# ScalarE normalises in the prologue, the second layernorm runs in halves, and attention values and sums share a bank

## The chip, the cores and the metric

The kernel runs on one core of one Trainium2 chip. The metric is the device time of one execution in microseconds (us), lower is better; the median of some runs is given. A core has five engines with queues of their own: TensorE (PE; its weight loads are PEld), VectorE (DVE), ScalarE (ACT), GpSimd (POOL) and SyncE (SP), which here only starts transfers. They wait for each other on semaphores alone. SBUF has 128 partitions; PSUM, which TensorE writes, has eight banks of 512 fp32 columns.

## The reference

Four sublayers on x of 4x256x256 (1,024 tokens, 256 wide), each on a layernorm and added back:

```
x = x + L0_xattn(layernorm(x), ctx)      # fp8-rounded activations times fp8-rounded ctx, per batch
x = x + L0_ffn(layernorm(x), ...)        # 32 experts, 4 a token, softmax of the 4 * 1.8, and one shared expert
x = x + L1_xattn(layernorm(x), ctx, ctx, gamma)   # 8 heads of 32, softmax(q k) v, times gamma
x = x + L1_ffn(layernorm(x), ...)        # 8 experts, 2 a token, and a shared expert of twice the width

def layernorm(x):  return (x - mean(x)) / sqrt(var(x) + 1e-5)
```

The first sublayer scales each block of 128 values by 448 over its largest magnitude, rounds to fp8, multiplies by the likewise rounded ctx and scales back. All the rest is fp32.

## The kernel before

x lies as eight tiles (NT) of 128 tokens in `x_sb`, the normalised x in `xn`. All engines' programs are written out by hand, and each engine works through its own in order.

**Prologue (0 to 57 us).** VectorE takes the statistics of x (`statistics`: L604, then L607), the largest magnitudes of ctx, and the inverse deviations of all tiles (`inverse_deviation`, L276 to L283: a Newton iteration of 11 small instructions on VectorE, 14 on POOL, each waiting for the one before). Then it scales ctx (L644) and finds the power of two for the rounding (L626, L627), and signals `c_mag`. POOL, which waits for it, adds and subtracts over 2048 columns (L389, L390): this rounds ctx to `wq`. VectorE meanwhile normalises the eight tiles (L612: one instruction a tile, minus the mean, times the inverse deviation), takes the block maxima of xn (L649, a reduction), then three small instructions (L650 to L652), a scale (L654) and `dq` (L657, eight small products), and rounds xn in two halves (L663, L626, L627, L665, L666). TensorE transposes the rounded halves (L930), ScalarE copies them out (printed at L463), TensorE multiplies (L938), and VectorE adds the scaled products into `x_sb` (L671, four instructions a tile). TensorE's product for tile t waits for tile t-2 there.

**Second layernorm and routing of layer 0 (57 to 110 us).** `layernorm(range(NT), xn_ready)` on VectorE: eight L604, eight L607, the inverse deviations, eight L612. TensorE transposes pairs of tiles (`turn_rows`, L988), ScalarE copies them (`router_copies`, L470) and TensorE makes the logits (L1004, four matmuls a tile); pairs 0 and 1 are turned first, then each next pair between the logits. Then VectorE picks the top four and builds the tables of slots; beside it TensorE, ScalarE and POOL run the first part of the shared expert (L964 up, L953 transposes, L975 down; POOL multiplies at L401 and adds at L406).

**Experts of layer 0 (110 to 252 us).** 48 tiles of 128 rows gathered by POOL's indirect transfers, TensorE busy throughout. Then POOL fetches the rows back (L431).

**Attention (the rows come back from 254 on; heads from 268 to 360 us).** VectorE combines the rows of tile t (L824), takes statistics and normalises; the inverse deviations of groups of two tiles are POOL's, by `by_pool`, whose keys are the heads g after which VectorE takes the statistics (the normalisation follows three heads later). 32 heads, four a tile: `scores` (L1123), the maximum (L848, VectorE), exponential (L560, ScalarE), transposes (`turn_p`, L1135), copy (L567, ScalarE). `values(t)` is four heads' values into bank 6 (L1148) and their sums into bank 7 (L1153). `tile_out(t)` on VectorE takes the reciprocal of the sums (L853), the product with gamma and the values (L855, signals `att_ready`) and adds to x (L858). `values(t)` waits for `att_ready` of t-1. In VectorE's order `tile_out(t)` stands after the maximum of head 4t+10 and before that of head 4t+11. The last two tiles' layernorm is VectorE's alone, and the routing of layer 1 begins.

**Experts of layer 1 (390 to 447 us)**, then rows back and the last combine.

## Time and profile before

| | us |
|---|---|
| median of 3 runs | 480.09 (478.62 to 483.44) |
| profiled execution | 486.58, span 484.8 |
| prologue, until x1 is complete | 57 |
| second layernorm and logits | 57 to 74 |
| routing and shared expert | 74 to 110 |
| experts of layer 0, rows back | 110 to 317 (the attention begins at about 268 within it) |
| rest of the attention | 317 to 360 |
| layer 1's experts | 360 to 485 |

A row of the timeline gives start and length in us, the engine, the line, the operation, what it writes and reads, how often, and in brackets how long the engine had stood idle and for whom. A piece of the chain gives start, length, engine, what is written and the line: it is what the end of the kernel hung on. Where several instructions stand in one row, its length runs from the first start to the last end.

### The profile page before, as it was taken

Reading aid. Unit: us, or ns where it says so; the run is one execution under the profiler, and the core shown is the slowest. Engines: PE = TensorE matmul, PEld = TensorE weight load, DVE = VectorE, ACT = ScalarE, POOL = GpSimd, SP = SyncE. Lnnn points to the kernel's source line nnn. Section 1 sums busy time; section 2 is a strip of 40 time slices with the busy share of each in tenths; the row PEclk is TensorE's granted clock in tenths of the full one; section 3 lists DMA queues with packets and bytes.
Section 4 is the critical chain, followed back from the end, with each engine's and each line's share of the span. In section 5 each row is a group of like instructions: output and inputs, shape, how many; then the busy total and the mean of one; then the engine's idle time right before and its main releaser. Section 6 shows DMA issues by size and latency. Waiting matters only on the chain.

```text
span 484.8 us, 8137 instructions
## 1 busy us (share of the span) xinstructions
PE 364.0 (75%) x2329; PEld 206.9 (43%) x2329; DVE 292.9 (60%) x807; ACT 179.3 (37%) x378; POOL 150.7 (31%) x219
## 2 busy tenths in 40 slices
PE   0002376789999999999960766888767989998993
PEld 0001174454545455455520434555454545544562
DVE  3999837933555555555544786678658235555273
ACT  1000030325555555555530434455612155553230
POOL 2250001443333333333106654542200433320362
PEclk9999999999999999999995557959865599999997
DMA  8998980054222222235522321296020113331242
GB/s 251 343 329 184 355 214 2 0 150 155 89 92 95 96 91 88 91 92 136 164 87 76 87 78 32 77 280 170 1 88 0 43 47 100 96 88 55 65 121 88
DMA packets 33371, 56.92 MB, mean 117 GB/s; under 512 B 4193, under 2 KB 20065, under 8 KB 33329
## 3 DMA queue, kind: packets, MB, share of 16 engines
q1 hardware_dynamic: 26145, 40.08, 26.8%
q0 software_dynamic: 5568, 15.21, 11.5%
q10 hardware_dynamic: 1616, 1.11, 0.8%
q8 instruction: 21, 0.34, 0.3%
q14 instruction: 21, 0.17, 0.1%
HBM read 44.33 MB, written 12.06 MB: 116 GB/s over the span
## 4 chain that ended last, share of the span: by engine, by line
PE 55%; DVE 20%; DMA 15%; issue 5%; POOL 3%; ACT 1%; DVEq 0%; SPq 0%; POOLq 0%; ACTq 0%
PE bank L1056 19%; DMA arena<-m_ys,back 13%; PE bank L1077 12%; PE bank L1067 5%; PE bank L964 4%; PE bank L1051 3%; DVE xn L612 3%; PE bank L975 2%; DVE arena L853 2%; PE bank L1004 2%; DVE st L604 2%; DVE x_sb L671 1%; DMA x_sb<-x 1%; POOL arena L431 1%; PE bank L953 1%
## 5 line engine op out<-in xcount | busy, mean ns | idle before, releaser
L1056 PE MATMUL bank<-arena,xT 128*64 x272 | 111.2, 491 | 1.1 <-ACT xT L528 1.1
L1059 PE MATMUL bank<-xn,xT 128*64 128x384 f32 (+1 forms) x272 | 111.2, 491 | 0.0
L418 POOL DMA_INDIRECT xg<-m_xn,tab x68 | 64.5, 949 | 121.6 <-PE bank L1051 118.9
L1077 PE MATMUL bank<-arena,hT 96*64 (+1 forms) x272 | 70.3, 380 | 2.8 <-DVE hT L792 2.7
L1080 PE MATMUL bank<-xn,hT 96*64 96x256 f32 (+1 forms) x272 | 70.4, 381 | 0.0
L431 POOL DMA_INDIRECT arena<-m_ys,back x48 | 47.5, 990 | 69.9 <-DMA m_ys<-ysb 40.5
L521 ACT ACTIVATE xn<-arena 128x768 f32 (+1 forms) x68 | 56.2, 827 | 22.0 <-issue 22.0
L811 DVE TENSOR_TENSOR hh<-sg,bank 128x192 f32<-128x192 f32 (+1 forms) x68 | 23.8, 349 | 59.4 <-issue 47.9
L1077 PEld LDWEIGHTS bank<-arena,hT 96*64 96x64 f32 (+1 forms) x272 | 34.9, 135 | 38.7 <-issue 28.3
L560 ACT ACTIVATE arena<-bank,att_nm 128x256 f32<-128x256 f32 x64 | 26.8, 477 | 52.4 <-DVE att_nm L848 52.4
L786 DVE COPY xn<-arena 96x512 f32 (+1 forms) x68 | 28.8, 423 | 23.0 <-issue 23.0
L964 PE MATMUL bank<-arena 128*128 128x352 f32 (+1 forms) x96 | 41.3, 560 | 0.0
L1056 PEld LDWEIGHTS bank<-arena,xT 128*64 128x64 f32 x272 | 31.4, 136 | 23.0 <-issue 13.9
L528 ACT ACTIVATE xT<-bank 128x256 f32<-128x256 f32 x68 | 26.0, 383 | 37.9 <-PE bank L1051 37.7
L799 DVE COPY ysb<-bank 128x256 f32<-128x256 f32 x68 | 28.9, 425 | 14.0 <-PE bank L1080 9.5
L1123 PE MATMUL bank<-arena,xn 32*128 32x256 f32 x128 | 22.8, 517 | 16.4 <-DVE xn L612 14.1
L1080 PEld LDWEIGHTS bank<-xn,hT 96*64 96x64 f32 (+1 forms) x272 | 34.9, 135 | 0.0
L542 ACT ACTIVATE sg<-bank 128x192 f32<-128x192 f32 (+1 forms) x68 | 22.2, 326 | 31.5 <-PE bank L1059 31.1
L824 DVE SCALAR_TENSOR_TENSOR x_sb<-arena,rw,x_sb 128x256 f32<-128x256 f32 x48 | 23.3, 485 | 17.2 <-DMA arena<-m_ys,back 16.1
L1135 PE MATMUL bank<-ident,arena 128*128 128x128 f32 x128 | 24.4, 333 | 12.2 <-ACT arena L567 9.7
L401 POOL TENSOR_TENSOR hh<-sg,up 128x192 f32<-128x192 f32 (+1 forms) x7 | 6.3, 902 | 81.8 <-ACT up L491 81.8
L1059 PEld LDWEIGHTS bank<-xn,xT 128*64 128x64 f32 x272 | 31.4, 136 | 0.0
(155 smaller groups left out, 577.2 us busy)
## 6 DMA issues: line engine op xcount, KB each, us to landing
arena<-w_gu SPq DMA_DIRECT2D x3, 3456.0 KB, 12.5
m_ys<-ysb SPq DMA_DIRECT2D x68, 128.0 KB
arena<-w_dn SPq DMA_DIRECT2D x3, 1728.0 KB, 20.6
arena<-w_gu SPq DMA_DIRECT2D x2, 1056.0 KB
m_xn<-xn SPq DMA_DIRECT2D x2, 1024.0 KB, 4.8
arena<-w_gu SPq DMA_DIRECT2D x2, 768.0 KB
arena<-w_gu SPq DMA_DIRECT2D x1, 1408.0 KB
xg<-m_xn,tab POOLq DMA_INDIRECT x68, 2.8
```

The lines of the kernel that those rows point to most:

```text
L418: nc.gpsimd.indirect_dma_start(out=xg[:, b, :], out_offset=None, in_=xn_d[L.name], in_offset=bass.IndirectOffsetOnAxis(ap=d["tab"][:, s:s ...
L431: nc.gpsimd.indirect_dma_start(out=back_rows[L.name][:, t, k, :], out_offset=None, in_=ys_d[L.name], in_offset=bass.IndirectOffsetOnAxis(a ...
L521: nc.scalar.activation(second[L.name][0][:, s % 2, :], arena[:, bass.ds(off, L.gu)], ACT.Copy).then_inc(m["gu_second"], 1)
L528: nc.scalar.activation(xT[:, s % 2].rearrange("p c m -> p (c m)"), bank[s % 2][:, 0:H], ACT.Copy).then_inc(m["xT_copied"], 1)
L560: nc.scalar.activation(pr_sb[:, g % 4, q, :], bank[g % 4][:, q * H:(q + 1) * H], ACT.Exp, bias=nm[:, g % 4, q:q + 1]).then_inc(p_raw, 1)
L786: V.tensor_copy(second[L.name][1], arena[0:L.J, bass.ds(off + L.gu, 2 * H)]).then_inc(m["dn_second"], 1)
L799: V.tensor_copy(ysb[:, s % BUFS, :], bank[6 + s % 2][:, 0:H]).then_inc(m["y_copied"], 1)
L964: ins = T.matmul(bank[4 + n % 2][:, 0:2 * J2], RS[L.name]["xT"][:, t, c, :], arena[:, at:at + 2 * J2], start=(c == 0), stop=(c == C - 1))
L1056: T.matmul(bank[2 + s % 2][0:BLOCK, 0:2 * J2], xT[:, s % 2, c, 0:BLOCK], arena[:, bass.ds(off + c * 2 * J2, 2 * J2)], start=(c == 0), stop ...
L1059: return T.matmul(bank[2 + s % 2][BLOCK:P, 0:2 * J2], xT[:, s % 2, c, BLOCK:P], gu2[:, s % 2, cols], start=(c == 0), stop=(c == C - 1), ti ...
L1077: T.matmul(bank[6 + s % 2][0:BLOCK, 0:H], hT[0:L.J, s % 2, a, 0:BLOCK], arena[0:L.J, bass.ds(off + L.gu + a * H, H)], start=(a == 0), stop ...
L1080: ins = T.matmul(bank[6 + s % 2][BLOCK:P, 0:H], hT[0:L.J, s % 2, a, BLOCK:P], dn2[:, a * H:(a + 1) * H], start=(a == 0), stop=(a == 1), ti ...
```

## The change

ScalarE gets `normalise(t, done)`: one Identity activation a tile, with the inverse deviation as scale and the negated mean times the deviation (`nmr`) as bias. In the prologue VectorE makes `nmr` of all tiles in one instruction after its inverse deviations, ScalarE normalises all eight tiles, and VectorE waits for that before its reduction.

The second layernorm goes in halves. After tile 4 of x1, VectorE takes the statistics of tiles 0 to 3, then goes on with tiles 5 to 7. POOL makes the deviations of tiles 0 to 3 and their `nmr` (two more instructions). VectorE takes statistics, deviations and `nmr` of tiles 4 to 7. ScalarE normalises each half and copies its transposed pairs. TensorE turns pairs 2 and 3 together, after the logits of pairs 0 and 1.

In the attention, values and sums of tile t are the two halves of bank 6 + t % 2, and `values(t)` waits for `att_ready` of t-2.

```diff
@@ -100,6 +100,7 @@
         ve = sb("ve", [P, NT])
         nt = sb("nt", [P, NT])
         rstd = sb("rstd", [P, NT])
+        nmr = sb("nmr", [P, NT])
         amc = sb("amc", [P, 16])
         amx = sb("amx", [P, 16])
         col16 = sb("col16", [P, 1])
@@ -249,10 +250,11 @@
             m["after"] = {n: sem(f"{L.name}_after_{n}") for n in
                           "g_done evacuated h_ready ht_done hT_copied d_done added".split()}
             M[L.name] = m
-        x2_ready, s_done, nm_ready, p_raw, p_ready, tp_done, pT_ready, av_done, x3_ready = (
-            sem(n) for n in ("x2_ready", "s_done", "nm_ready", "p_raw", "p_ready", "tp_done", "pT_ready", "av_done", "x3_ready"))
+        x2_ready, s_done, nm_ready, p_raw, tp_done, pT_ready, av_done, x3_ready = (
+            sem(n) for n in ("x2_ready", "s_done", "nm_ready", "p_raw", "tp_done", "pT_ready", "av_done", "x3_ready"))
         inv_ready, att_ready = sem("inv_ready"), sem("att_ready")
         stats_ready, rstd_ready = sem("stats_ready"), sem("rstd_ready")
+        ln_ready, ln1_done = sem("ln_ready"), sem("ln1_done")
         out_ready, stored = sem("out_ready"), sem("stored")
 
         block = es.enter_context(nc.Block())
@@ -390,6 +392,13 @@
             nc.gpsimd.tensor_tensor(wq.rearrange("p b k n -> p (b k n)"), v_c, c_c, ALU.subtract).then_inc(wq_ready, 1)
 
 
+            h = NT // 2
+            pool.wait_ge(stats_ready, 1)
+            inverse_deviation(nc.gpsimd, link, range(h), 1.0)
+            link(nc.gpsimd.tensor_tensor(nmr[:, 0:h], mv[:, 0:h, 0], rstd[:, 0:h], ALU.mult))
+            nc.gpsimd.tensor_scalar(nmr[:, 0:h], nmr[:, 0:h], -1.0, None, ALU.mult).then_inc(ln_ready, 1)
+
+
             def early_shared(L):
 
                 q, work = M[L.name]["early"], early_work[L.name]
@@ -436,7 +445,7 @@
                         after[1]()
 
             def deviations(i):
-                pool.wait_ge(stats_ready, i + 1)
+                pool.wait_ge(stats_ready, i + 2)
                 inverse_deviation(nc.gpsimd, link, *by_pool[sorted(by_pool)[i]])
                 pool.sem_inc(rstd_ready, 1)
 
@@ -457,6 +466,14 @@
             act.dma_start(rb0[:], router_b0.to_broadcast([P, L0.E])).then_inc(small_in, 16)
             act.dma_start(rw1[:], router_w1).then_inc(small_in, 16)
             act.dma_start(gamma_sb[:], gamma.to_broadcast([P, 1])).then_inc(small_in, 16)
+
+            def normalise(t, done):
+                nc.scalar.activation(xn[:, t, :], x_sb[:, t, :], ACT.Identity, bias=nmr[:, t:t + 1],
+                                     scale=rstd[:, t:t + 1]).then_inc(done, 1)
+
+            act.wait_ge(ln_ready, 1)
+            for t in range(NT):
+                normalise(t, ln1_done)
 
             for i in range(2):
                 act.wait_ge(xqT_done, i + 1)
@@ -542,7 +559,11 @@
                     nc.scalar.activation(sg[:, s % 2, 0:2 * L.J], bank[2 + s % 2][:, 0:2 * L.J],
                                          ACT.Silu).then_inc(m["sg_ready"], 1)
 
-            router_copies(L0, range(NT // 2))
+            for i in range(2):
+                act.wait_ge(ln_ready, i + 2)
+                for t in range(NT // 2 * i, NT // 2 * (i + 1)):
+                    normalise(t, M["m0"]["xn_ready"])
+                router_copies(L0, (2 * i, 2 * i + 1))
             early_shared(L0)
             after_shared(L0, 0, n_mid["m0"])
             act.wait_ge(w_early, 32 * -(-(L0.E - LATE) // EARLY))
@@ -636,7 +657,12 @@
             dve.wait_ge(amcT_done, 1)
             link(V.tensor_reduce(col16[0:16, :], bank[2][0:16, 0:P], AX.X, ALU.max))
             V.tensor_scalar(diag[0:16, :], ident[0:16, 0:16], col16[0:16, :], None, ALU.mult).then_inc(diag_ready, 1)
+            def negated_means(a, b, done):
+                V.scalar_tensor_tensor(out=nmr[:, a:b], in0=mv[:, a:b, 0], scalar=-1.0, in1=rstd[:, a:b],
+                                       op0=ALU.mult, op1=ALU.mult).then_inc(done, 1)
+
             inverse_deviation(V, link, range(NT), 1.0)
+            negated_means(0, NT, ln_ready)
             dve.wait_ge(amb_done, 1)
             link(V.tensor_scalar(safe_c[:], bank[3][:, 0:16], W_EPS, None, ALU.max))
             link(V.reciprocal(rin_c[:], safe_c[:]))
@@ -644,7 +670,7 @@
             link(V.tensor_tensor(ctx16, ctx16, rin_c[:].unsqueeze(2).broadcast_to([P, 16, P]), ALU.mult))
             power_of_two(c_c, v_c).then_inc(c_mag, 1)
 
-            link(normalise(range(NT)))
+            dve.wait_ge(ln1_done, NT)
             xn16 = v_x.rearrange("p (a n) -> p a n", n=P)
             link(V.tensor_reduce(amx[:], xn16, AX.X, ALU.max, apply_absolute_value=True))
             link(V.tensor_scalar(amx[:], amx[:], ACT_EPS, None, ALU.max))
@@ -674,6 +700,9 @@
                         if n == C - 1 and k < C - 1:
                             link(ins)
                 ins.then_inc(x1_ready, 1)
+                if t == NT // 2:
+                    dve.wait_ge(x1_ready, NT // 2)
+                    statistics(range(NT // 2)).then_inc(stats_ready, 1)
             dve.wait_ge(x1_ready, NT)
 
             def routing(L):
@@ -827,7 +856,10 @@
                         link(ins)
                 ins.then_inc(ready, 1)
 
-            layernorm(range(NT), M["m0"]["xn_ready"])
+            link(statistics(range(NT // 2, NT)))
+            inverse_deviation(V, link, range(NT // 2, NT), 1.0)
+            dve.wait_ge(ln_ready, 2)
+            negated_means(NT // 2, NT, ln_ready)
             routing(L0)
             after_shared(L0, 0, n_mid["m0"])
             dve.wait_ge(w_early, 32 * -(-(L0.E - LATE) // EARLY))
@@ -850,9 +882,9 @@
 
             def tile_out(t):
                 dve.wait_ge(av_done, t + 1)
-                V.reciprocal(inv_sb, bank[7][:, 0:H]).then_inc(inv_ready, 1)
+                V.reciprocal(inv_sb, bank[6 + t % 2][:, H:2 * H]).then_inc(inv_ready, 1)
                 dve.wait_ge(inv_ready, t + 1)
-                V.scalar_tensor_tensor(out=att_sb, in0=bank[6][:, 0:H], scalar=gamma_sb[:], in1=inv_sb,
+                V.scalar_tensor_tensor(out=att_sb, in0=bank[6 + t % 2][:, 0:H], scalar=gamma_sb[:], in1=inv_sb,
                                        op0=ALU.mult, op1=ALU.mult).then_inc(att_ready, 1)
                 dve.wait_ge(att_ready, t + 1)
                 V.tensor_tensor(x_sb[:, t, :], x_sb[:, t, :], att_sb, ALU.add).then_inc(x3_ready, 1)
@@ -995,7 +1027,10 @@
                 for i in range(turned, 2):
                     turn_rows(L, i)
                 for i in range(NT // 2):
-                    if i >= 1 and i + 1 < NT // 2:
+                    if L is L0 and i == 2:
+                        turn_rows(L, 2)
+                        turn_rows(L, 3)
+                    elif L is L1 and i >= 1 and i + 1 < NT // 2:
                         turn_rows(L, i + 1)
                     pe.wait_ge(m["rt_Tsb"], i + 1)
                     for t in (2 * i, 2 * i + 1):
@@ -1139,18 +1174,18 @@
             def values(t):
 
                 pe.wait_ge(pT_ready, HPT * (t + 1))
-                if t >= 1:
-                    pe.wait_ge(att_ready, t)
+                if t >= 2:
+                    pe.wait_ge(att_ready, t - 1)
                 for k in range(2):
                     for h in range(HPT):
                         rows = slice(h * HEAD, (h + 1) * HEAD)
                         at = (t % 2) * P + h * HEAD
-                        T.matmul(bank[6][rows, 0:H], vT[:, t // 2, k, at:at + HEAD], pT_sb[:, (HPT * t + h) % (2 * HPT), k, :],
+                        T.matmul(bank[6 + t % 2][rows, 0:H], vT[:, t // 2, k, at:at + HEAD], pT_sb[:, (HPT * t + h) % (2 * HPT), k, :],
                                  start=(k == 0), stop=(k == 1), tile_position=(0, h * HEAD))
                 for k in range(2):
                     for h in range(HPT):
                         rows = slice(h * HEAD, (h + 1) * HEAD)
-                        ins = T.matmul(bank[7][rows, 0:H], ones32[:, 0:HEAD], pT_sb[:, (HPT * t + h) % (2 * HPT), k, :],
+                        ins = T.matmul(bank[6 + t % 2][rows, H:2 * H], ones32[:, 0:HEAD], pT_sb[:, (HPT * t + h) % (2 * HPT), k, :],
                                        start=(k == 0), stop=(k == 1), tile_position=(0, h * HEAD))
                 ins.then_inc(av_done, 1)
 
```

## Rows read from the trace of the kernel before

**Rows 1.** Page, second part: tenths of DMA busy in 40 slices of 12.1 us.
```profile
DMA  8998980054222222235522321296020113331242
```

**Rows 2.** Chain that ended last, prologue: start us, length us, engine, tile, line.
```profile
21.62 11.02 DVE xn L612 x8
32.67 2.30 DVE amx L649
...
36.58 1.15 DVE xn L663
```

**Rows 3.** Timeline, end of x1, second layernorm and logits.
```profile
52.43 4.74 DVE L671 SCALAR_TENSOR_TENSOR x_sb<-bank,dq,x_sb 128x128 f32<-128x128 f32 x16 [0.98 <-PE bank L938]
...
57.20 2.71 DVE L604 BATCH_NORM_STATS2 st<-x_sb 128x6 f32<-128x256 f32 x8
...
60.62 0.17 DVE L276 TENSOR_SCALAR ve<-mv 128x8 f32<-128x8 f32 x1
...
62.84 2.68 DVE L612 TENSOR_SCALAR xn<-x_sb,mv,rstd 128x256 f32<-128x256 f32 x8
...
63.72 1.94 PE L988 MATMUL bank<-ident,xn 128*128 128x128 f32 x8 [8.21 <-DVE xn L612]
...
74.06 0.42 DVE L686 TENSOR_TENSOR lg<-bank,rb 128x256 f32<-128x256 f32 x1 [8.54 <-PE bank L1004]
```

**Rows 4.** Timeline, POOL and VectorE at the same time, prologue and routing.
```profile
21.71 4.59 POOL L389 TENSOR_TENSOR arena<-arena 128x2048 f32<-128x2048 f32 x1 [18.00 <-DVE arena L627]
26.38 4.49 POOL L390 TENSOR_TENSOR arena<-arena 128x2048 bf16<-128x2048 f32 x1
...
26.37 4.65 DVE L612 TENSOR_SCALAR xn<-x_sb,mv,rstd 128x256 f32<-128x256 f32 x1
...
35.48 0.17 DVE L652 TENSOR_SCALAR rin_x<-rin_x 128x16 f32<-128x16 f32 x1
...
77.06 1.22 DVE L707 TENSOR_TENSOR arena<-iota_e,idxf 128x1024 f32<-128x1024 f32 x1
...
77.41 1.32 POOL L401 TENSOR_TENSOR hh<-sg,up 128x192 f32<-128x192 f32 x1 [46.54 <-ACT up L491]
78.31 1.89 DVE L710 TENSOR_REDUCE m<-arena 128x256 bf16<-128x1024 f32 x1
```

**Rows 5.** Chain that ended last, one tile of the attention.
```profile
327.55 1.68 DVE arena L853
329.25 0.49 DVE arena L855
...
329.88 1.07 PE bank L1148 x16
...
334.16 0.67 DVE att_nm L848
```

**Rows 6.** Waits of TensorE, 285 to 356 us: total, times, longest.
```profile
PE bank L1148 <- DVE arena L855: 4.2, 5, 1.7
```

**Rows 7.** Groups of ScalarE by line: busy us, mean ns, idle before.
```profile
L560 ACT ACTIVATE arena<-bank,att_nm 128x256 f32<-128x256 f32 x64 | 26.8, 477 | 52.4 <-DVE att_nm L848 52.4
L528 ACT ACTIVATE xT<-bank 128x256 f32<-128x256 f32 x68 | 26.0, 383 | 37.9 <-PE bank L1051 37.7
```

**Rows 8.** Timeline of POOL, first and last of 14 instructions of one inverse deviation.
```profile
331.94 0.19 POOL L276 TENSOR_SCALAR ve<-mv 128x2 f32<-128x2 f32 x1 [9.01 <-DVE mv L607]
...
335.59 0.20 POOL L286 TENSOR_TENSOR rstd<-nt,rstd 128x2 f32<-128x2 f32 x1
```

**Rows 9.** Timeline, the last deviations by POOL and the last reciprocal.
```profile
347.17 0.19 POOL L276 TENSOR_SCALAR ve<-mv 128x2 f32<-128x2 f32 x1 [11.38 <-DVE mv L607]
...
352.73 1.76 DVE L853 RECIPROCAL arena<-bank 128x256 f32<-128x256 f32 x1 [0.73 <-PE bank L1153]
```

**Rows 10.** Chain that ended last, the shared expert of layer 0.
```profile
83.29 2.57 PE bank L964 x4
...
89.10 1.31 PE bank L964 x4
```

## Prediction

> **What bounds the kernel now.** I read the page first: TensorE is the busiest engine, but a share over the span says little here, since the kernel is a row of stages. In the two long expert stages TensorE is full, and the change touches no line of theirs: they only start earlier or later. Nor do transfers bound them: the DMA line is at 2 to 3 tenths there [rows 1]. So I went to the chain that ended last, for the stretches that the diff touches, and then to the timeline of each.
>
> In the prologue the chain is VectorE alone. Its largest piece is the first normalisation, 11.02 us for eight tiles of 128x256 [rows 2]. The same eight instructions in the second layernorm take 2.68 us [rows 3]. The reason is visible: POOL runs two additions over 2048 columns, 4.59 and 4.49 us, from 21.71 to 30.87, and the L612 that starts at 26.37 lasts 4.65 us, until POOL's second one ends [rows 4]. One L612 gets through between them. So VectorE was held by POOL for about 8.3 us.
>
> In the second layernorm VectorE does statistics of eight tiles, the inverse deviations and the normalisation while TensorE stands; then TensorE runs without a gap from 63.72 to 74.04 and VectorE stands until the logits are there [rows 3]. Nothing overlaps.
>
> In the attention, up to about 317, the combine of returned rows sets the pace; from then on the chain alternates: VectorE's reciprocal and product, TensorE's values and sums, transposes, scores, the next maximum. TensorE waited for the product L855 five times, 4.2 us in all, before L1148 [rows 5, 6].
>
> **Prologue.** The eight L612 leave VectorE (-11.02). One small instruction for the negated means comes in ahead, 0.20 with its gap, like the L276 of 0.17 [rows 3]; POOL's two additions move by the same 0.2 and end at 31.07. ScalarE does the eight tiles from about 16.3, where the deviations are ready. No SBUF to SBUF Identity of this shape is in the trace; the nearest rows are 0.38 and 0.48 us for 128x256 [rows 7]. That is 3.0 to 3.9 us, over at 20.2 at the latest, before L627 ends at 21.82: nothing on the path by either price. If it lasted longer than 5.5 us, all above that would be on the path, since L649 reads its output.
>
> But POOL is still there. VectorE now goes on at 21.82 with the reduction L649, 2.30 us, to 24.1, and then has L650, L651, L652 of 16 columns, and later the large product L663 [rows 2, 4]. What of these is held? In the routing stage POOL's product L401 starts at 77.41 while VectorE has two inputs in SBUF (L707), and ends 0.45 after L707, though VectorE's reduction L710 is by then running [rows 4]. So a reduction leaves POOL alone, a product with two SBUF inputs and a one-source L612 do not. I take L650 and L652 as held like L612 (same kind, smaller): L650 passes in the gap at 26.5, L652 at 31.07 and ends at 31.26. It ended at 35.65 before [rows 4]. **Gain 4.4 us.** If the small ones pass freely, L663 still waits for 31.07, where it started at 36.58: gain 5.5, less if the eight small products ahead of it are held too. Both bounds are near.
>
> The Trainium skill, page SBUF — State Buffer, section Who interferes with whom, speaks against the full gain: a VectorE instruction in a two-port mode (tensor_scalar among them) or with two SBUF inputs and a GpSimd instruction that reads SBUF exclude each other for a whole instruction, and a reduction never takes part. The rows above agree as far as they go; they do not show a held product on VectorE's side. By the rule the sum is the 4.4 taken; without it, it would be the rival of 10.8 below.
>
> **Second layernorm in halves.** I keep the axis of before here and take the 4.4 off at the end. Tile 4 of x1 is done at 52.43 + 4.74/4 = 53.6. VectorE then does four L604 and four L607: half of the 3.42 from 57.20 to 60.62, 1.7 us, to 55.3 [rows 3]. POOL takes 14 instructions of the deviations and two more for the negated means: fourteen took 331.94 to 335.79, 0.275 each [rows 8], so 16 take 4.4, to 59.8. Four elements against two a row should not matter. The cover for this: VectorE finishes tiles 5 to 7 meanwhile (3.6 us, to 58.9), whose L671 has one SBUF input only. Then the other four statistics, 1.7, to 60.6, its own inverse deviations, 2.22 (60.62 to 62.84 before), the negated means, 0.2: 63.1 with the gaps. VectorE's own part is 0.2 longer than before.
>
> ScalarE normalises tiles 0 to 3 from 59.8, the first pair at 60.7, all at 61.5 (0.42 each). Its four tiles of the second half follow at 63.1 and are there at 64.8. The copies of transposed rows, 0.6 each, sit between them. TensorE has 16 transposes and 32 logit matmuls, 10.3 us in all [rows 3]. It can start at 60.7, turns pairs 0 and 1 (to 62.5), does their logits (3.4, to 65.9), and by then the second half is there; it goes on without a gap to 60.7 + 10.3 = 71.0, against 74.04. **Gain 3.0 us.** Behind ScalarE's waits only the two copies of the first half are queued, and they need TensorE's turns, which are earlier. Bounds: if the first half brings nothing, TensorE starts at 63.1 + 0.85 and ends 0.2 later than before (loss 0.2); if the first half were free, it ends with 63.1 + 0.85 + two turns 1.8 + 3.3 = 69.1 (gain 4.9).
>
> After the logits all follows in its order: routing, shared expert, tables. The third block of weights is issued behind the second quantised half, so 4.4 earlier; the DMA shares of the page are at nothing between 73 and 97 us, so the weights are no bound at 110 [rows 1].
>
> **Attention.** Values and sums of tile t go to one bank, and wait for the product of t-2, which is long over. From the end of the scores at 326.87 to that of the next at 334.16 the chain was 0.67 maximum, 1.68 reciprocal, 0.49 product, 0.14, 1.93 values and sums, 1.22 turns, 1.11 scores: 7.3 [rows 5]. Without the wait, TensorE finishes values 0.87 earlier, but its next turn but one needs the exponential of a head whose maximum VectorE takes only after the whole of `tile_out`: 0.67 + 1.68 + 0.49 + 0.44 + 0.69, exponential 0.84, turn 0.63, scores 1.11, gaps 0.25 = 6.8. So 0.5 a tile, not 0.87: the wait goes to VectorE's queue. For tiles 3 and 4 that is 0.7 + 0.5. Tile 5 gains nothing more (VectorE and ScalarE are the chain there). At the end the largest wait, 1.7 [rows 6], goes, but VectorE's order puts the normalisation of tiles 4 and 5 ahead of the last `tile_out`, and this waits for POOL's deviations, which start at 347.17 and take the 3.85 of [rows 8], to 351.0. They move by 1.2 with the rest, to 349.8; L612 follows for 0.75 with a gap of 0.2, and L853 can start at 350.8, against 352.73 [rows 9]. **Gain 1.9 us.** Bounds: with no shift of the statistics, L853 starts at 352.0 (0.7); without POOL's bound all the 4.2 of waits comes out.
>
> **Sum.** 4.4 + 3.0 + 1.9 = 9.3 us. The profiled execution took 486.6 us (span 484.8) and would take 477.3; the rows of the touched stages are engine work, so I take the same off the median: 480.1 - 9.3 = 470.8.
>
> **Rivals.** (a) VectorE is not held by POOL outside L612: L650 to L663 run freely and the whole 11.02 less 0.2 goes. 10.8 + 3.0 + 1.9 = 15.7, 464.4. For it: no held small instruction and no held product is in the rows. Against: L707 held L401. Chance 0.08.
> (b) The halves bring nothing: POOL's deviations are held up, or ScalarE's order is, and the first logits start with the second half. 4.4 - 0.2 + 1.9 = 6.1, 474.0. POOL would have to need 63.1 - 59.8, some 3 us, more than its rows say. Chance 0.12.
> (c) TensorE's clock comes up earlier. The matmul rows L964 show 2.57 us for four at 83.29 and 1.31 at 89.10 [rows 10], the second of TensorE's two levels against the first, 1.2 GHz and then 2.4. Denser work ahead of it could bring two of the slow steps to the fast price, 1.3 to 2.1 each: 467. Chance 0.08.
> (d) The other side, slower: the same clock comes up late. In the first shared-expert steps each step at 1.2 GHz costs 1.26 more on L964 [rows 10], and by proportion 0.84 on the down products, which have 256 columns for 384: 2.1 in all. There are eight steps; from 4.4 slow ones on, the gain of 9.3 is gone, and with all eight the time is 480.1 - 9.3 + 16.9 = 487.7. For it: those stages do run slow once TensorE has stood. Against: the pattern of work ahead of them is not thinner than before. Chance 0.05.
> (e) Prologue and attention both at the low end, or the held L650 slips behind POOL's second addition and more: gain under 4.8, about 476. Chance 0.05.
>
> **Numbers.** The forecast has 0.62, its own range 468 to 473. The range of all is 465 to 476: it leaves out most of (a) and (d) and part of (e), and holds the low bound with a little noise. One per cent, 4.8 us, is about what can be told from no change. Faster by more: all of the forecast, (a), (b), (c), less a little noise: 0.88. Within: 0.08. Slower: 0.04.
>
> **What would show it.** Right: no L612 in VectorE's prologue, eight ScalarE activations there over before L627 ends; a small tensor_scalar of over 4 us on VectorE near 26.7, ending with POOL's second addition; logits done near 66.6; no wait of L1148 for L855; the L612 ahead of the last reciprocal waiting for POOL. Wrong: L663 starting before POOL ends (a), ScalarE's first half after VectorE's second (b), L964 at 2.57 after the first steps (d), or a stage outside of these three whose length changed.

## The result, and the profile after

The changed kernel takes 474.3 us (473.51 to 478.02, four runs) beside 481.45 of the kernel before: ratio 0.9862, 95% interval 0.9832 to 0.9892. By the ratio that is 6.6 us less, between 5.2 and 8.1 by the ends of the interval; the two medians alone are 7.15 apart. The forecast was 9.3 us less, 470.8, with its own range at 468 to 473: the time lies outside of that one and inside the range of all, 465 to 476. Executions more than 1.5% above the fastest of their kernel are left out of the ratios and intervals here and below, but not out of the medians. The profiled execution has a span of 471.8 us, 13.0 under that of before. Of that profile of before one must know that its 486.58 us are 5.1 above the kernel's median, while the 473.51 of the changed kernel's are the fastest of its four; and 4.4 of the 13.0 lie in a stretch that takes one of two lengths in profiles of one and the same changed kernel, as shown below.

Line numbers move: L612 is now L633 on VectorE and L471 on ScalarE, L649 to L652 are L675 to L678, L663 is L689, L988 is L1020, L1004 is L1039, L848 is L880, L853 is L885, L855 is L887, L1123 is L1158, L1135 is L1170, L1148 and L1153 are L1183 and L1188, L964 is L996.

The prologue, timeline of the changed kernel, against [rows 2, 4]:

```profile
16.87 4.04 ACT L471 ACTIVATE xn<-x_sb,nmr,rstd 128x256 f32<-128x256 f32 x8 [11.67 <-DVE nmr L661]
...
22.19 2.28 DVE L675 TENSOR_REDUCE amx<-xn 128x16 f32<-128x2048 f32 x1
22.35 4.50 POOL L391 TENSOR_TENSOR arena<-arena 128x2048 f32<-128x2048 f32 x1 [18.64 <-DVE arena L648]
24.50 2.39 DVE L676 TENSOR_SCALAR amx<-amx 128x16 f32<-128x16 f32 x1
...
26.93 4.50 POOL L392 TENSOR_TENSOR arena<-arena 128x2048 bf16<-128x2048 f32 x1
27.21 4.25 DVE L678 TENSOR_SCALAR rin_x<-rin_x 128x16 f32<-128x16 f32 x1
...
32.29 1.22 DVE L689 TENSOR_TENSOR xn<-xn,rin_x 128x1024 f32<-128x1024 f32 x1
```

ScalarE's eight tiles end at 20.9, before L648 does. Two instructions of 16 columns take 2.39 and 4.25 us: each ends with one of POOL's additions. L689 starts at 32.29, where its like started at 36.49 before: 4.2 us earlier, though VectorE's first reduction, over ctx, began 0.6 us later in this execution (9.98 for 9.40).

The second layernorm, timeline, against [rows 3]:

```profile
51.29 0.20 POOL L278 TENSOR_SCALAR ve<-mv 128x4 f32<-128x4 f32 x1 [19.86 <-DVE mv L628]
...
55.61 0.23 POOL L399 TENSOR_SCALAR nmr<-nmr 128x4 f32<-128x4 f32 x1
55.87 2.07 ACT L471 ACTIVATE xn<-x_sb,nmr,rstd 128x256 f32<-128x256 f32 x4 [8.38 <-POOL nmr L399]
...
57.11 2.01 PE L1020 MATMUL bank<-ident,xn 128*128 128x128 f32 x8 [4.10 <-ACT xn L471]
...
67.75 0.42 DVE L715 TENSOR_TENSOR lg<-bank,rb 128x256 f32<-128x256 f32 x1 [8.86 <-PE bank L1039]
```

The logits are there at 67.75, not 74.06. TensorE starts 1.27 us after the end of POOL's last instruction (1.24 after ScalarE's first) and needs 10.6 us.

The attention: the chain that ended last, one tile, against [rows 5], and the waits of TensorE (total, times, longest) from 275 to 350 us, against [rows 6]:

```profile
318.92 1.68 DVE arena L885
...
320.62 0.49 DVE arena L887
...
321.13 0.44 DVE x_sb L890
...
321.60 0.70 DVE att_nm L880
...
322.69 0.47 ACT arena L581
323.16 0.50 ACT arena L588
...
323.79 0.63 PE bank L1170 x4
324.42 1.11 PE bank L1158 x8
325.53 0.67 DVE att_nm L880
```

```profile
PE bank L1170 <- ACT arena L588: 12.9, 9, 2.9
PE bank L1158 <- issue: 1.3, 1, 1.3
PE bank L1183 <- ACT arena L588: 0.3, 1, 0.3
```

No wait of the values for VectorE's product is left. The turns wait instead, for ScalarE's copy. From one maximum to the next (318.25 to 325.53) it is 7.28 us, where the kernel before had 7.29.

The end of the attention, timeline, against [rows 9]:

```profile
342.35 0.19 POOL L288 TENSOR_TENSOR rstd<-nt,rstd 128x2 f32<-128x2 f32 x1
342.70 0.74 DVE L633 TENSOR_SCALAR xn<-x_sb,mv,rstd 128x256 f32<-128x256 f32 x2 [1.64 <-POOLq L450]
...
343.70 1.76 DVE L885 RECIPROCAL arena<-bank 128x256 f32<-128x256 f32 x1 [0.26 <-PE bank L1188]
```

VectorE waits 1.64 us for POOL there, as forecast, and 0.26 for TensorE behind it: here the last values and sums ran at 1.2 GHz (1.62 and 1.95 us), and TensorE, not POOL, ended last. In the second profile of the changed kernel they took 1.07 and 1.05 us, and POOL alone was the bound:

```profile
344.35 0.74 DVE L633 TENSOR_SCALAR xn<-x_sb,mv,rstd 128x256 f32<-128x256 f32 x2 [1.65 <-POOLq L450]
...
345.00 1.75 DVE L885 RECIPROCAL arena<-bank 128x256 f32<-128x256 f32 x1
```

### The profile page after: what moved, and what is told of

It reads as the page before. It is cut to its first block, busy times and chain, and to the rows that moved or that the text cites. A ratio compares the mean times of both kernels' runs of the same rounds, so it can differ in the third digit from the quotient of the medians.

```text
span 471.8 us, 8154 instructions
## 1 busy us (share of the span) xinstructions
PE 361.3 (77%) x2329; PEld 203.4 (43%) x2329; DVE 285.9 (61%) x793; ACT 187.3 (40%) x394; POOL 155.1 (33%) x235
## 4 chain that ended last, share of the span: by engine, by line
PE 60%; DVE 20%; DMA 9%; issue 5%; ACT 2%; POOL 2%; DVEq 0%; SPq 0%; ACTq 0%; POOLq 0%
PE bank L1091 19%; PE bank L1112 13%; DMA arena<-m_ys,back 7%; PE bank L996 6%; PE bank L1102 5%; PE bank L1007 4%; PE bank L1086 3%; DVE arena L885 2%; PE bank L1039 2%; PE bank L985 2%; DVE att_nm L880 2%; DMA x_sb<-x 2%; PE bank L1170 1%; DVE st L625 1%; PE bank L1158 1%
## 5 line engine op out<-in xcount | busy, mean ns | idle before, releaser
L581 ACT ACTIVATE arena<-bank,att_nm 128x256 f32<-128x256 f32 x64 | 26.8, 477 | 52.0 <-DVE att_nm L880 52.0
L996 PE MATMUL bank<-arena 128*128 128x352 f32 (+1 forms) x96 | 39.9, 545 | 0.0
L1170 PE MATMUL bank<-ident,arena 128*128 128x128 f32 x128 | 24.2, 331 | 15.5 <-ACT arena L588 12.9
L1158 PE MATMUL bank<-arena,xn 32*128 32x256 f32 x128 | 21.8, 500 | 16.5 <-DVE xn L633 14.2
L853 DVE SCALAR_TENSOR_TENSOR x_sb<-arena,rw,x_sb 128x256 f32<-128x256 f32 x48 | 23.3, 485 | 14.6 <-DMA arena<-m_ys,back 13.3
L1102 PE MATMUL bank<-ident,hh 128*96 128x128 f32 (+1 forms) x136 | 28.7, 292 | 0.5 <-DVE hh L840 0.5
```

The lines of the kernel that those rows point to most:

```text
L996: ins = T.matmul(bank[4 + n % 2][:, 0:2 * J2], RS[L.name]["xT"][:, t, c, :], arena[:, at:at + 2 * J2], start=(c == 0), stop=(c == C - 1))
L1102: ins = T.transpose(bank[4 + s % 2][0:L.J, a * P:(a + 1) * P], hh[:, s % 2, a * L.J:(a + 1) * L.J], ident[:])
L1170: ins = T.transpose(bank[4 + g % 2][:, (2 * k + q) * P:(2 * k + q + 1) * P], pr_sb[:, g % 4, q, k * P:(k + 1) * P], ident[:])
```

## Where the 13 us of the two profiles lie

This table is read from the timelines of eight profiles: when the routing's first instruction on VectorE finds the logits, when the first expert matmul starts, when POOL's first row comes back, the last reciprocal of the attention, layer 1's logits, its first expert matmul, the span. "a", "b", "c" and the rest are the experiments below.

| kernel | logits 0 | expert 0 | rows back | last reciprocal | logits 1 | expert 1 | span | logits 1 to expert 1 |
|---|---|---|---|---|---|---|---|---|
| before | 74.1 | 110.6 | 254.5 | 352.7 | 363.9 | 391.7 | 484.8 | 27.8 |
| after | 67.8 | 104.1 | 248.3 | 343.7 | 354.9 | 378.3 | 471.8 | 23.4 |
| after, again | 67.4 | 105.3 | 249.5 | 345.0 | 356.2 | 383.7 | 476.3 | 27.5 |
| a prologue alone | 69.2 | 105.9 | 250.1 | 346.5 | 357.7 | 381.1 | 474.8 | 23.4 |
| c attention alone | 74.0 | 110.5 | 254.4 | 350.5 | 361.7 | 389.5 | 482.6 | 27.8 |
| a and b | 67.3 | 103.8 | 247.9 | 344.0 | 355.2 | 382.9 | 477.2 | 27.7 |
| f short additions | 61.0 | 97.6 | 241.8 | 336.8 | 348.0 | 375.7 | 469.8 | 27.7 |
| g additions moved | 62.2 | 100.8 | 244.8 | 342.2 | 353.4 | 378.4 | 471.4 | 25.0 |

In every profile VectorE's first reduction, over ctx, starts at a slightly different time: 9.40 us before, 9.98 after, 9.56 after again, 9.32 in a, 9.71 in b, 9.49 in a and b. Counted from there the logits are at 64.7 before and in c, 59.9 in a, 62.6 in b, 57.8 in all three of after, after again and a and b. So the prologue's part gives 4.8 us at the logits and the halves 2.1.

The last column takes one of two values in most profiles: 23.4 (after, a and, below, h, i, k, m) or 27.5 to 27.8 (before, b, c, after again, a and b, f, j). The changed kernel has shown both. The three kernels without the prologue's change (before, b, c) have one profile each and showed only the long one, so it is not shown that they can draw the short one. What differs is TensorE's clock. Stretches of the kernel before and of the changed one follow; the columns are the stretch, its length, the busy time (and count) of PE, PEld, DVE, ACT and POOL, the granted clock, the DMA share and GB/s.

```profile
368.40:372.00 3.60, 2.60 (x23) 1.96 (x24) 2.57 (x17) 0.38 (x1) 0.00 (x0) 0.50 0.00 0
...
381.00:385.00 4.00, 3.22 (x8) 2.04 (x8) 0.34 (x1) 0.72 (x3) 2.79 (x3) 0.50 0.34 98
```

```profile
359.40:363.00 3.60, 2.62 (x23) 1.95 (x24) 2.57 (x18) 0.38 (x1) 0.00 (x0) 0.50 0.00 0
363.00:367.00 4.00, 3.26 (x11) 1.91 (x10) 3.93 (x19) 1.29 (x4) 1.28 (x2) 0.80 0.00 0
367.00:372.00 5.00, 4.10 (x30) 2.63 (x29) 2.44 (x14) 1.08 (x3) 2.55 (x3) 1.00 0.06 15
```

In the same place of the program, some 9 us later on the clock of before, the granted clock stays at 0.50 (1.2 GHz) until the end of the shared expert's steps in the first, and is at 2.4 GHz by 367 us in the second. That is 4.4 of the 13.0 us. The rest, 8.6, is 9.0 ahead of layer 1's logits, with 0.4 lost behind its first expert matmul. The two profiles of before and after again, both with the long stretch, have spans 8.5 us apart.

## The experiments

All ratios are to the kernel before on the same chip.

| kernel | median us | ratio | 95% interval |
|---|---|---|---|
| a prologue alone | 478.02 | 0.9909 | 0.9878 to 0.9941 |
| b halves alone | 481.57 | 0.9987 | 0.9954 to 1.0020 |
| c attention alone | 481.12 | 0.9989 | 0.9954 to 1.0024 |
| after, again | 475.87 | 0.9869 | 0.9818 to 0.9919 |
| a and b | 475.71 | 0.9892 | 0.9847 to 0.9937 |
| f short additions | 471.91 | 0.9817 | 0.9774 to 0.9860 |
| g additions moved | 471.61 | 0.9781 | 0.9736 to 0.9826 |
| h exponential one head later | 474.07 | 0.9838 | 0.9793 to 0.9883 |
| j late normalisation | 477.44 | 0.9870 | 0.9808 to 0.9932 |
| k both of g and j | 470.59 | 0.9779 | 0.9736 to 0.9821 |
| m k with TensorE filled | 470.41 | 0.9793 | 0.9751 to 0.9835 |
| i both of g and h | 470.00 | 0.9709 | 0.9626 to 0.9792 |

**The prologue alone.** Edit of the kernel before:

```diff
...
+            negated_means(0, NT, ln_ready)
...
-            link(normalise(range(NT)))
+            dve.wait_ge(ln1_done, NT)
```

> The kernel before with ScalarE's normalisation in the prologue alone; the second layernorm and the attention stay as they were. Theory (POOL's two additions hold VectorE's small instructions and its product, so 8.3 us of holding shrink to 6.3 us and the eight normalisations go): x1 complete about 4.4 us earlier, the time 4 to 5 us under the kernel before, ratio about 0.990. Rival (the gain is given back before the experts begin, because the routing waits for something that does not move): x1 earlier by as much, but the first expert tile and the time within 1 us of before.

x1 is complete at 52.3 against 57.2, the logits at 69.2 against 74.1, the first expert matmul 4.7 us earlier. Ratio 0.9909: 4.4 us (2.8 to 5.9). The theory holds, its rival (given back before the experts) falls. This profile drew the short stretch of layer 1, so its span says nothing beyond the marks ahead of it.

**The halves alone.** Edit of the kernel before: the diff's parts of the second layernorm, the ScalarE `normalise` and the order of the turns.

> The kernel before with the second layernorm in halves alone (POOL's deviations of tiles 0 to 3, ScalarE's normalisation, turns of pairs 2 and 3 together). Theory: the logits are done 2 to 3 us earlier than in the kernel before, and the time is 2 to 3 us less, ratio about 0.995. Rival (the time from x1 to the logits hardly changes, the profile of the changed kernel had its gain from elsewhere): logits within 0.5 us, ratio 1.000.

The logits are at 72.3 against 74.1, 1.8 us earlier. Of this lead 1.6 is left at the first expert matmul, 1.0 at the first row back, and none at layer 1's logits (364.1 against 363.9): the experts take 144.5 us for 143.9, and from the first row to the first reciprocal it is 43.3 for 42.1. This execution took 485.9 us, 4.3 above the kernel's median of 481.57, so it doesn't tell whether the halves or the execution took the lead back. The time is 0.6 us less, with an interval of 1.6 to each side: the 1.8 is within it, and so is nothing; the 0.995 of the theory is just outside it (0.9954 to 1.0020). The direct look at the logits refutes the rival for that spot; what the whole time gains of it this run doesn't tell.

**The attention alone.** Edit of the kernel before:

```diff
...
-                if t >= 1:
-                    pe.wait_ge(att_ready, t)
+                if t >= 2:
+                    pe.wait_ge(att_ready, t - 1)
...
-                        T.matmul(bank[6][rows, 0:H], vT[...
+                        T.matmul(bank[6 + t % 2][rows, 0:H], vT[...
...
```

> The kernel before with the shared banks of the attention alone. Theory (VectorE's and ScalarE's order take over most of the 4.2 us of waits): no wait of TensorE for the product of the tile before, the maximum after each tile at the same spacing of about 7.3 us, the stretch from the first returned rows to layer 1's logits 2 to 3 us shorter, ratio about 0.995. Rival (what this stretch gained in the changed kernel came from TensorE's clock in that one execution, not from the wait): the stretch as long as before, ratio 1.000.

The last reciprocal comes 2.2 us earlier, but the whole time is 0.5 us less with 1.7 to each side. The spacing of the reciprocals tells more, since VectorE no longer waits for returned rows behind the third. From the third to the last it is 34.5 us in all four kernels with the old attention (before, a, b, a and b: 34.46 to 34.49), and 32.5 to 33.6 in five profiles with the new one (after 33.45, after again 32.46, this 33.56, f 33.03, g 33.55). So the change gives about 1.3 us, 0.9 to 2.0 from profile to profile. Most of that scatter is TensorE's clock: it stood at 1.2 GHz for 4.4 to 6.9 us of the spacing from the third reciprocal to the fourth. Where this time is the same, the old attention and the new differ by 0.4 us there: 8.78 in a and 8.38 in this kernel with 6.0 us at 1.2 GHz, 8.99 in b and 8.58 in the changed kernel with 6.5. Between tiles 3 and 4 it gives nothing: 7.28 to 7.29 us in all nine. The stretch that the expectation named, from the first returned row to layer 1's logits, is 107.3 us for 109.4, 2 less, as the theory had it, but the kernels a and "a and b" have 107.6 and 107.3 with the old attention, so it measures more than the attention. The wait for the product is gone, as expected. The expected 0.995 is just outside the interval. The gain is real, but hardly more than half of what was expected.

**The changed kernel again.**

> The changed kernel once more, for a second profile and a tighter interval. Theory: the engine work accounts for 4.8 us in the prologue, 2.1 in the second layernorm and 2.8 in the attention, 9 to 10 us in all, ratio 0.980; the other 4 us of difference between the two first profiles lie in layer 1's shared expert and are TensorE's clock, which differs from execution to execution. Rival (something gives 3 us back): ratio 0.986 again, and a stretch of this profile longer than the same stretch of the kernel before.

Ratio 0.9869, as the rival had it. Yet no stretch of this profile is longer than in the kernel before by more than 1.4 us: that is the routing of layer 0, 37.9 us against 36.6, one step of the shared expert more at 1.2 GHz. The stretch of layer 1 is 27.5 here, as the theory said, where it was 23.4 in the first profile of the same kernel. The theory's 0.980 is outside the interval (0.9818 to 0.9919): of its three terms, 4.8, 2.1 and 2.8, the first two stand in all profiles and the third was too large.

**Prologue and halves, old attention.** Edit of the changed kernel: the attention's lines as they were.

> The changed kernel with the attention as it was before (values in bank 6, sums in bank 7, wait for the product of the tile before): prologue and halves only. Theory (the halves are worth the 1.8 us seen at the logits): about 2 us under the prologue alone, ratio 0.987, and the changed kernel is 1.5 to 2.5 us faster than this. Rival (the halves give their gain back behind the logits): logits 1.8 us earlier than with the prologue alone, but the first expert tile or the end no earlier, ratio 0.991.

Against the prologue alone the logits are 1.9 us earlier, the first expert matmul 2.2, the first row 2.2, layer 1's logits 2.5. So here the halves keep their 2 us to layer 1, which in b alone they did not, and then this profile drew 27.7 and that of the prologue alone 23.4. The waits of TensorE show the old attention's:

```profile
PE bank L1183 <- DVE arena L887: 6.3, 6, 1.9
```

The whole time, 0.9892, is between the two expectations, with both in its interval. It does not tell this kernel from the changed one either (0.9862 and 0.9869), where 1.5 to 2.5 us were expected.

**POOL's additions over 256 columns.** Edit of the changed kernel:

```diff
-            link(nc.gpsimd.tensor_tensor(v_c, v_c, c_c, ALU.add))
+            link(nc.gpsimd.tensor_tensor(v_c[:, 0:H], v_c[:, 0:H], c_c[:, 0:H], ALU.add))
...
+            act.wait_ge(c_mag, 1)
+            nc.scalar.activation(wq.rearrange("p b k n -> p (b k n)")[:, H:], v_c[:, H:], ACT.Copy).then_inc(wq_ready, 1)
...
```

> The changed kernel with POOL's two additions over 256 of the 2048 columns; ScalarE copies the other 1792 unrounded, so the rounding of ctx is left out there. This takes away what holds VectorE in the prologue and leaves VectorE's instructions alone. Theory (VectorE's small instructions and products are held by POOL's additions, 2.2 and 4.1 us in the changed kernel's profile): the two small instructions behind the reduction take 0.17 us each, x1 is complete 6.3 us earlier than in the changed kernel, the time about 6 us less, ratio to the kernel before about 0.973. Rival (those two instructions are long for another reason, such as waiting for ScalarE's output or for the reduction's write): they stay above 2 us, ratio 0.987.

Timeline of this kernel:

```profile
21.87 0.73 POOL L391 TENSOR_TENSOR arena<-arena 128x256 f32<-128x256 f32 x1 [18.14 <-DVE arena L650]
22.68 0.73 POOL L392 TENSOR_TENSOR arena<-arena 128x256 bf16<-128x256 f32 x1
24.01 0.17 DVE L678 TENSOR_SCALAR amx<-amx 128x16 f32<-128x16 f32 x1
...
24.51 0.17 DVE L680 TENSOR_SCALAR rin_x<-rin_x 128x16 f32<-128x16 f32 x1
...
25.52 1.22 DVE L691 TENSOR_TENSOR xn<-xn,rin_x 128x1024 f32<-128x1024 f32 x1
```

The two instructions that took 2.39 and 4.25 take 0.17 each. The reduction ran beside POOL at its full 2.28 in both kernels. x1 is complete at 47.9 against 54.3 in the second profile of the changed kernel: 6.4 us. The holding is shown, and its price is 6.3 us. The median is 4 us under the changed kernel's second series, less than the 6 expected, and the expected ratio of 0.973 is just below the interval. The two profiled executions, which both drew the long stretch of layer 1, are 6.5 us apart in their spans (469.8 and 476.3); where the series lose 2 us of that is open.

**POOL's additions moved beside other work.** Edit of the changed kernel (POOL, then VectorE):

```diff
+            nc.gpsimd.tensor_tensor(v_c[:, 0:hw], v_c[:, 0:hw], c_c[:, 0:hw], ALU.add).then_inc(wq_added, 1)
+            pool.wait_ge(xq_ready, 2)
+            link(nc.gpsimd.tensor_tensor(v_c[:, hw:], v_c[:, hw:], c_c[:, hw:], ALU.add))
...
+            dve.wait_ge(wq_added, 1)
+            V.tensor_tensor(wq.rearrange("p b k n -> p (b k n)")[:, 0:hw], v_c[:, 0:hw], c_c[:, 0:hw],
...
```

> The changed kernel with POOL's work of the prologue moved: it adds 1024 columns beside VectorE's reduction, VectorE subtracts these itself (one product-like instruction of 1.2 us), and POOL does the other 1024 columns beside the sums of x1, which have one SBUF input. Theory: nothing of VectorE is held; 6.3 us of holding go for 1.2 us of work, x1 complete 5 us earlier than in the changed kernel, ratio to the kernel before about 0.976. Rival (POOL also holds the reduction or the sums of x1): these get longer by 2 us or more, and the gain is under 2 us.

Timeline of this kernel:

```profile
21.49 2.28 DVE L680 TENSOR_REDUCE amx<-xn 128x16 f32<-128x2048 f32 x1
21.66 2.34 POOL L393 TENSOR_TENSOR arena<-arena 128x1024 f32<-128x1024 f32 x1 [17.95 <-DVE arena L653]
24.11 1.23 DVE L683 TENSOR_TENSOR arena<-arena 128x1024 bf16<-128x1024 f32 x1 [0.34 <-POOL arena L393]
25.25 0.17 DVE L685 TENSOR_SCALAR amx<-amx 128x16 f32<-128x16 f32 x1
...
36.98 4.73 DVE L706 SCALAR_TENSOR_TENSOR x_sb<-bank,dq,x_sb 128x128 f32<-128x128 f32 x16
37.14 2.34 POOL L395 TENSOR_TENSOR arena<-arena 128x1024 f32<-128x1024 f32 x1 [13.13 <-DVE ysb L701]
```

Neither the reduction nor the sums of x1 (one input in PSUM) are longer beside POOL. x1 is complete at 49.1, 5.1 us before the changed kernel's second profile. The ratio is 0.9781 where 0.976 was expected, about 4 us under the changed kernel. The interval ends at 0.9826; those of the changed kernel's two series begin at 0.9832 and 0.9818, so by g alone the second is not quite cleared. The three kernels below that contain the same edit (i, k, m) have 0.9709, 0.9779 and 0.9793.

**ScalarE's order.** Edit of the changed kernel:

```diff
...
-                if g + 3 < nheads:
-                    softmax_exp(g + 3)
+                if g + 2 < nheads:
+                    softmax_exp(g + 2)
```

> The changed kernel with ScalarE's order in the attention changed: the exponential of head g+2, not g+3, stands behind the copy of head g, so the copy that frees a bank for the next turn comes before the exponential that VectorE delays. Theory (in the changed kernel the removed wait went to ScalarE's queue: exponential, then copy, then turn): the spacing of the maxima after a tile falls from 7.3 to about 6.8 us, 1 to 1.5 us over the attention, ratio to the kernel before about 0.984. Rival (the spacing is VectorE's own or TensorE's): it stays at 7.3, ratio 0.987; if ScalarE falls behind, it rises.

Timeline of this kernel:

```profile
318.72 1.97 PE L1170 MATMUL bank<-ident,arena 128*128 128x128 f32 x8
...
322.63 1.93 PE L1183 MATMUL bank<-arena 128*32 128x256 f32 x16
...
328.89 1.75 DVE L885 RECIPROCAL arena<-bank 128x256 f32<-128x256 f32 x1
...
333.03 0.84 ACT L581 ACTIVATE arena<-bank,att_nm 128x256 f32<-128x256 f32 x2 [1.98 <-DVE att_nm L880]
...
333.92 0.66 PE L1170 MATMUL bank<-ident,arena 128*128 128x128 f32 x4 [0.36 <-ACT arena L581]
...
336.28 1.75 DVE L885 RECIPROCAL arena<-bank 128x256 f32<-128x256 f32 x1
```

Two spacings answer differently. That from the fifth reciprocal to the sixth falls from 7.93 to 7.39 us, 0.5 less, as the theory has it: TensorE was at 2.4 GHz there, and its turn now waits for the exponential (L581) and no longer for the copy behind it. The one before it, 7.29 in all earlier profiles, is 9.46: TensorE ran its turns, values and sums there at 1.2 GHz (1.93 for the values, against 1.07 at 2.4 GHz), so it says nothing of the order. In sum this profile loses more than it gains: from the third reciprocal to the last it is 34.95 us, against 33.45 and 32.46 in the changed kernel's two. The ratio, 0.9838, is what the theory had, but the rival's 0.987 lies in the interval too. The same edit on top of g:

> The changed kernel with POOL's work of the prologue moved and with ScalarE's exponential one head later in its order. The reciprocals of tiles 3 and 4 of the attention stand 7.28 to 7.29 us apart in nine profiles, with and without the shared banks; in the one profile with ScalarE's other order TensorE ran them at 1.2 GHz. Theory (in the changed kernel the chain there is maximum, output of the tile, maximum, exponential, copy, turn, scores): with TensorE at 2.4 GHz, 6.7 to 6.9 us. Rival (something else fixes the spacing): 7.3 again.

The two spacings are 9.42 and 7.38: the same again. So the sentence "6.7 to 6.9 at 2.4 GHz" was not tested. The clock comes up later with this order in both profiles, at 326 us in h against 317 in the changed kernel and at 321 in this one against 315 in g; why was not tried. From the third reciprocal to the last it is 34.91 us, 1.4 more than in g. The ratio is 0.9709, the lowest of all, but it rests on three executions, one of them 464.69, and its interval (0.9626 to 0.9792) overlaps those of g, k and m; the median, 470.00, is 0.4 us under m's and 0.6 under k's. That this order is worth anything in the whole time is not shown.

**The last normalisation moved.** Edit of the changed kernel:

```diff
...
             tile_out(NT - 1)
+            dve.wait_ge(rstd_ready, len(by_pool))
+            normalise(by_pool[28][0], M["m1"]["xn_ready"])
             dve.wait_ge(x3_ready, NT)
```

> The changed kernel with the normalisation of tiles 4 and 5 for layer 1 put behind the last output of the attention on VectorE, so that VectorE no longer waits there for POOL's deviations. Theory (the removed wait came back in part as this wait for POOL): the last two reciprocals stand 4.3 to 4.6 us apart instead of 5.0 to 5.6, unless TensorE runs at 1.2 GHz there, when it is its values and sums that bound; up to 1 us less, ratio to the kernel before about 0.985. Rival (TensorE's last values bound that spot anyway): spacing unchanged, ratio 0.987.

Timeline of this kernel:

```profile
341.57 1.05 PE L1191 MATMUL bank<-arena,ones 128*32 128x256 f32 x16
...
342.76 1.76 DVE L885 RECIPROCAL arena<-bank 128x256 f32<-128x256 f32 x1 [1.32 <-PE bank L1191]
...
345.41 0.73 DVE L633 TENSOR_SCALAR xn<-x_sb,mv,rstd 128x256 f32<-128x256 f32 x2
```

The last two reciprocals stand 4.03 us apart instead of 5.0 to 5.6, a little less than the 4.3 to 4.6 expected, and VectorE now waits for TensorE. This profile had TensorE at 2.4 GHz there, and so its nearest neighbour is the changed kernel's second, with 5.00: in these two POOL's deviations were the bound, as forecast. But 0.5 comes back at once, since the two L633 now stand ahead of the last layernorm: from the last reciprocal to layer 1's logits it is 11.7 us against 11.2. In the whole time nothing of it shows, here or together with g:

> The changed kernel with both improvements: POOL's work of the prologue moved, and the late normalisation. Theory: 5 us from the prologue and 0.5 to 1 us from the attention under the changed kernel, about 469.5 us, ratio to the kernel before about 0.975. Rival (the 5 us are given back by the clock or by transfers behind the logits): ratio 0.982 or more, with the first expert tile 5 us earlier but a later stretch longer.

0.9779 against g's 0.9781. In its profile TensorE had 1.2 GHz at the last values and sums (1.93 and 1.91 us), VectorE waited 3.01 us for them, and the spacing is 5.72: at that clock moving the normalisation gives nothing.

**TensorE filled.** Edit of k (three matmuls in all):

```diff
...
+                        for _ in range(2 if i == 2 else 0):
+                            T.matmul(bank[5][:], ident[:], RS["m1"]["xT"][:, 0:2].rearrange("p t c m -> p (t c m)"), start=True, stop=True)
...
```

> The kernel of both improvements with three more fp32 matmuls of 512 columns into an unused bank on TensorE in layer 1's routing, two where it waits for the last pair of tiles and one where it waits for the mask; they compute nothing that is used. In the profiles so far the stretch from layer 1's logits to its first expert tile takes 23.4 us where the granted clock is back at 1.00 by 367 us, and 27.5 to 27.8 us where it stays at 0.50 until 385. Theory (what TensorE has done before sets which of the two it is): this stretch at 23.4 us or less in the profile, and fewer long runs among the timed ones, median 2 us under the kernel without the extra matmuls. Rival (it is chance, or fixed by something else): the stretch as often 27.7 as before, and the median unchanged or up to 2 us worse by the work added.

Stretches of this kernel, 350 to 354 (logits done, waiting) and 354 to 360:

```profile
350.00:354.00 4.00, 2.55 (x10) 1.30 (x9) 3.03 (x30) 2.06 (x4) 0.55 (x1) 1.00 0.00 0
354.00:360.00 6.00, 4.04 (x26) 2.75 (x27) 4.79 (x27) 0.38 (x1) 0.00 (x0) 0.58 0.00 0
```

The clock is at 2.4 GHz where the others have 0.50, and falls again after. The stretch is 23.4 us, which k reached as well. The median, 470.41, is k's 470.59 within the intervals, where 2 us less were expected. That filling helps is not shown.

## Why the prediction was right, and where it was off

**The number and the mechanisms.** The change is faster by more than one per cent, as forecast, the prologue and the halves do what they were said to do, and the attention does it in part. But the time, 474.3, misses the forecast's own range of 468 to 473, and it is close to the number of rival (b), 474.0, whose mechanism did not come: the logits show the halves at work. That the number fell inside the range of all is owed to the width of that range. The sum was too high by 0.9 us for the halves and by 0.6 for the attention, too low by 0.4 for the prologue, and some of the gain that the marks show is not found in the whole time.

**The prologue, forecast 4.4, measured 4.8 at x1 and the logits, counted from the first reduction, and 4.4 (2.8 to 5.9) in the whole time.** The step "L650 and L652 are held like L612" is confirmed by their 2.39 and 4.25 us, and by f, where they take 0.17. Rival (a) falls with it. The 0.4 more are small terms: the instruction for the negated means cost VectorE next to nothing, since L644's like still started at 16.80 us in a for 16.81 before; POOL's first addition took 4.50 us for 4.59; and L652's like ended with POOL's second addition, at 30.8, not 0.2 behind it. ScalarE's price was above its own range, 0.50 a tile for 0.38 to 0.48, and cost nothing, since the eight end at 20.9 under L648.

The Trainium skill, page SBUF — State Buffer, section Who interferes with whom, had the rule: here it agrees, for 16 columns as for 2048, with the reduction outside it (2.28 us beside POOL). That section also says that a VectorE instruction with at most one SBUF input, outside the two-port modes, does not contend; g's 4.73 us for the sums, with POOL's addition beside them, agree.

**The halves, forecast 3.0, measured 2.1 at the logits.** The mechanism is right: TensorE starts on POOL's half and goes on without a gap. Four terms were too small. POOL 4.6 for 4.4; statistics in the middle 1.8 for 1.7; the first pair 1.27 behind POOL for 0.9, as ScalarE's tile costs 0.50 and there is a gap; TensorE 10.6 for 10.3. Together 0.9 us, which is what is missing. What was gained at the logits stays to layer 1 in a and b against a, but not in the profile of b alone, an execution 4.3 us above its median. Rival (b) falls at the logits; that the whole time keeps the 2 us is not shown, since neither ratio (0.9987 for b, 0.9892 for a and b beside 0.9909 for a) tells it from nothing.

**The attention, forecast 1.9, measured about 1.3 (0.9 to 2.0).** The step that failed is "0.5 a tile": I put the next turn behind the exponential of the head that VectorE had delayed, 6.8 us in all. The turn also waits for ScalarE's copy that frees its bank, and this copy stands behind that exponential in ScalarE's order. Its 0.50 is in the chain above, and the spacing is 7.28 for 7.29: at tile 4 the change gives nothing. What came, came at tile 3 and at the end. At tile 3 it is 0.8 as a mean (the fourth reciprocal stands 7.93 to 8.58 us behind the third, 8.78 to 9.20 with the old attention), but only 0.4, for the 0.7 forecast, where TensorE was at 1.2 GHz for equally long; the other 0.4 hangs on where its slow stretch fell. The end gives 0.5: the last two spacings are 9.3 to 10.0 us together, 10.05 to 10.5 with the old attention. The forecast named POOL's deviations as the bound of the end. VectorE waits 1.6 us for them in all five, but only in the second profile of the changed kernel are they what ended last; in the other four TensorE's values and sums ran at 1.2 GHz for most of their 3.3 to 3.6 us, and VectorE waited another 0.26 to 0.57 for them. With the old attention they ran at 2.4 GHz in all four profiles. So the clock took back a part of what the missing wait gave, which the forecast had no term for. By ScalarE's order 0.5 a tile is to be had at 2.4 GHz, shown at the sixth reciprocal only.

**The sum.** 4.8 + 2.1 + 1.3 = 8.2 by the marks, against 6.6 (5.2 to 8.1) and 6.3 (3.9 to 8.8) in the two series: just above the first interval, inside the second. Of the difference 0.3 is found: the experts of layer 0 take 144.2 us from first matmul to first row in a, a and b, the changed kernel, f, h and j, and 143.9 before, in c, and in the four kernels with POOL's additions moved (g, i, k, m); why is not known. The rest is less than what the clock does from execution to execution, and stays open.

**Rivals (c) and (d), the clock.** Neither came as put: in layer 0 the slow steps are the same two in most profiles, one more in two (37.9 in the changed kernel's second and in k) and more in g (38.6). But the clock moved layer 1's routing and shared expert by 4.4 us, a place that I had not looked at for it, though the page's row of the granted clock was low there before: the steps of layer 1 were in view only as "only start earlier". The same sentence of the prediction has the DMA line at 2 to 3 tenths in the expert stages; in layer 0's it also stands at 4 and 5 [rows 1], which changes nothing in the sum.

## What to carry to other kernels

Before work is taken off VectorE because POOL holds it, look what VectorE does next: the hold passes to the next instruction that the pair cannot do at once, here two of 16 columns, and the gain is the difference of two holds. Try POOL's large elementwise work beside VectorE's reductions and beside its instructions with one input in PSUM; here that gave 5.1 us at x1 and about 4 in the whole time, on top of what the change gave.

When a wait is taken from an in-order engine, write out the chain of the next round with every wait of each instruction, the buffer's release too, and through every engine's own order. A wait for a bank that is freed by a copy behind the late instruction is as late as that instruction.

Two profiles of one kernel differed by 4.5 us here, and those of before and after by 13.0 where the series differ by 6.6. Compare the same marks in several kernels that share the stage, counted from an early instruction that the change does not touch: for the prologue and the halves they agree to 0.1 us. Where they do not agree, as in the attention, give the spread, and look at the granted clock in each.

## What was not expected of the hardware

- An instruction of 16 columns on VectorE was held for 4.25 us by a POOL addition of 4.50, though alone it takes 0.17. POOL's additions took 0.73, 2.34 and 4.50 us for 256, 1024 and 2048 columns.
- The activation Identity from SBUF to SBUF with scale and bias for each partition took 0.50 us for 128x256, against 0.38 for a copy from PSUM of the same size [rows 7].
- TensorE's granted clock stayed at 0.50 until about 10 us behind layer 1's logits in one profile (after, 364.6) and until about 23 us behind them in another (before, 386.6), with the same 23 matmuls in 2.6 us in between. The stretch took 23.4 or 27.5 to 27.8 us in 13 of 14 profiles, 4.4 us between.
